# A graph network's convolution layer: W2 multiplied behind the neighbour sum, the residual product beside the last sweep

## What is computed

```python
deg = segment_sum(ones, dst); dinv = rsqrt(deg)      # with a self loop for each node
h = x @ W                                            # layer 2
agg = segment_sum(h[src] * (dinv[src] * dinv[dst])[:, None], dst) + b
x = layernorm(x + leaky(agg, 0.1) + x)
...
aggr = segment_sum(x[src] + edge_attr @ edge_w + edge_b, dst) / max(cnt, 1)     # layer 3
h = (1 + eps) * x + aggr
out = relu(h @ w1 + b1) @ w2 + b2 + (x @ res_w + res_b)
```

## Time and profile before

| | |
|---|---|
| three timed runs | 8806.70, 8809.26, 8819.43 us; median 8809.26 |
| profiled execution | 8815.13 us, span 8813.4 us |
| busy in the span | PE 2052.3 (23%), DVE 5593.5 (63%), ACT 3091.3 (35%), POOL 6086.1 (69%) |
| t2, first gather of its sums to first gather of l2s | 6208.9 to 6411.1 us |
| l2s, first to last gather | 6411.1 to 7450.2 us |
| t3, first gather to first gather of l3s | 7474.4 to 7590.0 us |
| l3s, first to last gather | 7590.0 to 8630.1 us |

### The profile page before, as it was taken

The page is one execution under the profiler, slowest core; times in us unless marked ns, Lnnn a source line. Parts: engine busy times, 40 slices in busy tenths (PEclk is TensorE's granted clock), DMA queues, the critical chain, the costliest instruction groups (busy, mean ns, idle before and its releaser), DMA issues. The chain is left out here.

```text
span 8813.4 us, 60467 instructions
## 1 busy us (share of the span) xinstructions
PE 2052.3 (23%) x16367; PEld 1898.9 (22%) x16367; DVE 5593.5 (63%) x10159; ACT 3091.3 (35%) x3341; POOL 6086.1 (69%) x6351
## 2 busy tenths in 40 slices
PE   5776634555400000810000720000500000300002
PEld 5666634555300000710000610000400000200002
DVE  7665546766599998868888468888632222432225
ACT  6333312333266665345555345555200000100002
POOL 2777777777777775667776367777267776577773
PEclk5555555555555555955555865555555555555556
DMA  4621114444366665656665556666333332233331
GB/s 131 216 60 42 37 51 134 130 133 135 115 204 219 218 216 180 206 195 216 216 216 201 170 192 216 216 216 211 93 95 105 105 105 95 78 106 105 105 105 56
DMA packets 496250, 1288.01 MB, mean 146 GB/s; under 512 B 153909, under 2 KB 262024, under 8 KB 428968
## 3 DMA queue, kind: packets, MB, share of 16 engines
q1 hardware_dynamic: 236712, 755.83, 24.3%
q0 software_dynamic: 229248, 473.78, 18.5%
q10 hardware_dynamic: 29952, 54.54, 2.4%
HBM read 731.68 MB, written 551.98 MB: 146 GB/s over the span
## 5 line engine op out<-in xcount | busy, mean ns | idle before, releaser
L1405 POOL DMA_INDIRECT l_swp_G<-table,KVI x1664 | 1576.4, 947 | 512.3 <-issue 506.7
L1661 POOL DMA_INDIRECT l2s_G<-table,OTHI x832 | 786.7, 946 | 388.1 <-issue 253.3
L1661 POOL DMA_INDIRECT l3s_G<-table,OTHI x832 | 787.7, 947 | 301.5 <-issue 253.3
L1065 POOL DMA_INDIRECT arrived<-plc_QS,plc_idx x832 | 812.3, 976 | 253.5 <-issue 244.3
L1065 POOL DMA_INDIRECT slots<-REC,plc_idx x832 | 798.5, 960 | 273.1 <-issue 251.7
L1150 POOL DMA_INDIRECT l_G<-table,OTHI x832 | 790.1, 950 | 256.1 <-issue 253.0
L904 PE MATMUL plc_pr<-plc_seen,plc_otf 128*128 128x49 f32 x3328 | 861.5, 414 | 12.4 <-DVE plc_seen L674 12.4
L904 PEld LDWEIGHTS plc_pr<-plc_seen,plc_otf 128*128 128x128 f32 x3328 | 846.6, 326 | 32.1 <-issue 31.9
L1508 DVE SCALAR_TENSOR_TENSOR l_swp_QS<-l_swp_QS,KEEP,l_swp_QX 128x128 f32<-128x128 f32 x1664 | 588.3, 354 | 45.9 <-DMA l_swp_QX<-queries 8.6
L1617 PE MATMUL l_swp_AW<-l_swp_ET,ones 128*128 128x512 f32 x4 | 4.1, 1140 | 2155.2 <-DVE l_swp_ET L1597 2155.2
L1287 DVE TENSOR_TENSOR_SCAN l_X<-l_AW,l_X 128x2244 f32<-128x2244 f32 x104 | 502.5, 4831 | 3.6
(11 more groups left out here) (491 smaller groups left out, 9633.2 us busy)
## 6 DMA issues: line engine op xcount, KB each, us to landing
sums<-l_ROW SPq DMA_DIRECT2D x104, 1088.0 KB, 4.6
l_swp_QX<-queries SPq DMA_DIRECT2D x104, 1088.0 KB, 8.3
sums<-l_swp_ROW SPq DMA_DIRECT2D x104, 1088.0 KB, 5.2
queries<-plc_zrow SPq DMA_DIRECT2D x55, 1088.0 KB
plc_QX<-queries SPq DMA_DIRECT2D x104, 544.0 KB, 4.2
l_A<-arrived SPq DMA_DIRECT2D x52, 1056.0 KB, 7.7
sums<-l3s_ROW SPq DMA_DIRECT2D x52, 1032.0 KB
plc_low<-low_rows ACTq DMA_DIRECT2D x208, 256.0 KB, 3.6
```

Of the source, the lines that this page charges most:

```text
L1065: pool.indirect_dma_start(out=slots, out_offset=bass.IndirectOffsetOnAxis(ap=idx[:, c % IB, j:j + 1], axis=0), in_=g.REC[:, c * CH + j, :] ...
L1405: pool.indirect_dma_start(out=G[:, c % GR, j, :], out_offset=None, in_=table, in_offset=bass.IndirectOffsetOnAxis(ap=index[:, c * CK + j:c ...
L1661: pool.indirect_dma_start(out=G[:, c % GR, j, :], out_offset=None, in_=table, in_offset=bass.IndirectOffsetOnAxis(ap=g.OTHI[:, c * CK + j: ...
```

## The change

Table2 now holds X * dinv rather than (X @ W2) * dinv, and the sweep sums rows without weights. In t2 the transposes, copies, products and own_rows of 49 blocks go; one pass of a group makes OWN (part 3 of norm_part), and LAG is 2. In t3 the sum, scaled and with the self loop added, is turned and multiplied by W2 with b as the bias row, and only then bent, added and normalised. The residual product moves into l3s, one block beside each chunk. To make room for its two PSUM buffers, S holds 12 slots of a chunk (SP_) instead of 16, and the sums of slots 12 to 15 are written straight to ROW. The seven passes that added b in l2s go.

```diff
+SP_ = 12
...
-        S = s.ps("S", [P, 2, CK, D])
+        S = s.ps("S", [P, 2, SP_, D])
...
+                sp.dma_start(wr[:, :], a.res_w).then_inc(loaded, 16)
+                sp.dma_start(br[:, 0, :], a.b2.rearrange("(o d) -> o d", o=1)).then_inc(loaded, 16)
+                sp.dma_start(br[:, 1, :], a.res_b.rearrange("(o d) -> o d", o=1)).then_inc(loaded, 16)
                 sp.dma_start(vec[:, :], row_of(a.edge_b)).then_inc(vec_ok, 16)
                 sp.dma_start(eps[:, :], a.eps.rearrange("(o d) -> o d", o=1).to_broadcast([P, 1])).then_inc(vec_ok, 16)
-            else:
-                sp.dma_start(vec[:, :], row_of(a.b2g)).then_inc(vec_ok, 16)
...
-                act.activation(ROW[:, c % 2, 0:CK - 1, 0:D], S[:, c % 2, 0:CK - 1, :], ACT.Copy).then_inc(rowed, 1)
+                act.activation(ROW[:, c % 2, 0:SP_, 0:D], S[:, c % 2, :, :], ACT.Copy).then_inc(rowed, 1)
+                if weight and 0 <= c - 1 < NB:
+                    n = c - 1
+                    act.wait_ge(turned, n + 1)
+                    if n >= 2:
+                        act.wait_ge(made, n - 1)
+                    act.activation(xt[:, n % 2, :], pt[:, 0:P], ACT.Copy).then_inc(copied, 1)
+                if weight and 0 <= c - 2 < NB:
+                    n = c - 2
+                    act.wait_ge(made, n + 1)
+                    act.activation(g.RES[:, n, :], pb[:, 0:D], ACT.Copy).then_inc(kept, 1)
...
             link(v.memset(ROW[:, 1, CK - 1, :], 0.0))
             if weight:
+                v.wait_ge(loaded, 48)
+                v.tensor_tensor(br[:, 0, :], br[:, 0, :], br[:, 1, :], ALU.add).then_inc(joined, 1)
                 link(v.tensor_tensor_scan(WS[:, :], g.KEEP[:, :], g.WEIGHT[:, :], 0.0, ALU.mult, ALU.add))
...
-                    line = vec[:, :].rearrange("p (o d) -> p o d", o=1).to_broadcast(wide)
                     if weight:
+                        line = vec[:, :].rearrange("p (o d) -> p o d", o=1).to_broadcast(wide)
                         link(v.tensor_tensor(g.BASE[:, cut, :], cols3(share[:, cut]).to_broadcast(wide), line, ALU.mult))
                         link(v.scalar_tensor_tensor(out=g.BASE[:, cut, :], in0=g.X[:, cut, :], scalar=eps[:, 0:1],
                                                     in1=g.BASE[:, cut, :], op0=ALU.mult, op1=ALU.add))
                     else:
                         own = g.OWN[:, cut, :]
                         link(v.tensor_tensor(own, own, cols3(g.DINV[:, cut]).to_broadcast(wide), ALU.mult))
-                        link(v.tensor_tensor(own, own, line, ALU.add))
...
-                    before = S[:, b, j - 1, :] if j else ROW[:, 1 - b, CK - 1, 0:D]
-                    after = S[:, b, j, :] if j < CK - 1 else ROW[:, b, CK - 1, 0:D]
+                    before = S[:, b, j - 1, :] if 0 < j <= SP_ else ROW[:, b if j else 1 - b, (j - 1) % CK, 0:D]
+                    after = S[:, b, j, :] if j < SP_ else ROW[:, b, j, 0:D]
...
+            def residual(n):
+                pe.wait_ge(copied, n + 1)
+                if n >= 1:
+                    pe.wait_ge(kept, n)
+                pe.matmul(pb[:, 0:D], xt[:, n % 2, :], wr[:, :], start=True, stop=False)
+                pe.matmul(pb[:, 0:D], g.ones[0:1, :], br[:, 0, :], start=False, stop=True).then_inc(made, 1)
+
+            if weight:
+                pe.wait_ge(joined, 1)
+                for n in range(NB):
+                    if n >= 1:
+                        pe.wait_ge(copied, n)
+                    pe.transpose(pt[:, 0:P], g.X[:, n, :], g.ident[:, :]).then_inc(turned, 1)
+                    if n >= 1:
+                        residual(n - 1)
+                residual(NB - 1)
             pe.wait_ge(rowed, NCK)
...
-    LAG = 11 if gcn else 3
+    LAG = 2 if gcn else 3
...
-            if gcn:
-                sp.dma_start(W2[:, :], a.W2).then_inc(rel_ok, 16)
-            else:
+            if not gcn:
...
-                n = s_ - 11
-                if gcn and 0 <= n < NB and n % GT == GT - 1:
-                    sp.wait_ge(owned, n + 1)
-                    sp.dma_start(rows(g.table2)[:, group(n // GT), :], g.OWN[:, group(n // GT), :]).then_inc(stored[0], 16)
+                G = (s_ - 8) // GT
+                if gcn and (s_ - 8) % GT == 0 and 0 <= G < NG:
+                    sp.wait_ge(owned, G + 1)
+                    sp.dma_start(rows(g.table2)[:, group(G), :], g.OWN[:, group(G), :]).then_inc(stored[0], 16)
...
-            def own_rows(n):
-                v.wait_ge(made2, n + 1)
-                v.tensor_scalar(g.OWN[:, n, :], pg[:, 0:D], g.DINV[:, n:n + 1], None, ALU.mult).then_inc(owned, 1)
+                elif j == 3:
+                    v.tensor_tensor(g.OWN[:, group(G), :], x, cols3(g.DINV[:, group(G)]).to_broadcast(wide), ALU.mult).then_inc(owned, 1)
...
-                    if 0 <= s_ - 10 < NB:
-                        own_rows(s_ - 10)
...
-            def copy_x(n):
-                act.wait_ge(turned2, n + 1)
-                if n >= 2:
-                    act.wait_ge(made2, n - 1)
-                act.activation(xt[:, n % 2, :], pf[:, 0:P], ACT.Copy).then_inc(copied2, 1)
...
-            def turn_next(n):
-                if n % GT == 0:
-                    pe.wait_ge(normed2, n // GT + 1)
-                if n >= 1:
-                    pe.wait_ge(copied2, n)
-                pe.transpose(pf[:, 0:P], g.X[:, n, :], g.ident[:, :]).then_inc(turned2, 1)
-
-            def make_own(n):
-                pe.wait_ge(copied2, n + 1)
-                if n >= 1:
-                    pe.wait_ge(owned, n)
-                pe.matmul(pg[:, 0:D], xt[:, n % 2, :], W2[:, :], start=True, stop=True).then_inc(made2, 1)
...
-                    if s_ == 8:
-                        pe.wait_ge(rel_ok, 16)
-                    if 0 <= s_ - 8 < NB:
-                        turn_next(s_ - 8)
-                    if 0 <= s_ - 9 < NB:
-                        make_own(s_ - 9)
...
-            sp.dma_start(wr[:, :], a.res_w).then_inc(loaded, 16)
-            sp.dma_start(br[:, 0, :], a.b2.rearrange("(o d) -> o d", o=1)).then_inc(loaded, 16)
-            sp.dma_start(br[:, 1, :], a.res_b.rearrange("(o d) -> o d", o=1)).then_inc(loaded, 16)
+            sp.dma_start(wr[:, :], a.W2).then_inc(loaded, 16)
+            sp.dma_start(br[:, :], a.b2g.rearrange("(o d) -> o d", o=1)).then_inc(loaded, 16)
...
             def first(G):
+                y = NV[:, group(G), :]
+                v.wait_ge(fetched[G], 16 * GT)
+                link(v.tensor_tensor(y, y, cols3(g.DINV[:, group(G)]).to_broadcast(wide), ALU.mult))
+                v.tensor_tensor(y, y, g.OWN[:, group(G), :], ALU.add).then_inc(summed, 1)
+
+            def middle(G):
                 x, y = g.X[:, group(G), :], NV[:, group(G), :]
                 m = st[:, G % 2, :, :]
-                v.wait_ge(fetched[G], 16 * GT)
-                link(v.tensor_tensor(y, y, cols3(g.DINV[:, group(G)]).to_broadcast(wide), ALU.mult))
-                link(v.tensor_tensor(y, y, g.OWN[:, group(G), :], ALU.add))
+                v.wait_ge(kept, (G + 1) * GT)
                 link(v.scalar_tensor_tensor(out=y, in0=y, scalar=0.1, in1=y, op0=ALU.mult, op1=ALU.max))
...
-            v.wait_ge(loaded, 48)
-            v.tensor_tensor(br[:, 0, :], br[:, 0, :], br[:, 1, :], ALU.add).then_inc(summed, 1)
+            first(0)
             for G in range(NG + 1):
+                if G + 1 < NG:
+                    first(G + 1)
                 if G < NG:
-                    first(G)
+                    middle(G)
                 if G >= 1:
                     second(G - 1)
...
-                act.activation(g.RES[:, n, :], pb[:, n % 2, 0:D], ACT.Copy).then_inc(kept, 1)
-
-            for G in range(NG + 1):
-                if G < NG:
-                    act.wait_ge(centered, G + 1)
-                    act.activation(SQ[:, G % 2, :, :], g.X[:, group(G), :], ACT.Square).then_inc(squared, 1)
-                if G >= 1:
-                    act.wait_ge(spread, G)
-                    act.activation(st[:, (G - 1) % 2, 2, :], st[:, (G - 1) % 2, 1, :], ACT.Sqrt).then_inc(rooted, 1)
-                if G >= 2:
-                    for n in range((G - 2) * GT, (G - 1) * GT):
-                        copy(n)
-                        if n >= 1:
-                            keep(n - 1)
-            for n in range((NG - 1) * GT, NB):
-                copy(n)
-                keep(n - 1)
-            keep(NB - 1)
+                act.activation(NV[:, n, :], pb[:, n % 2, 0:D], ACT.Copy).then_inc(kept, 1)
+
+            def close(G):
+                act.wait_ge(centered, G + 1)
+                act.activation(SQ[:, G % 2, :, :], g.X[:, group(G), :], ACT.Square).then_inc(squared, 1)
+
+            def root(G):
+                act.wait_ge(spread, G + 1)
+                act.activation(st[:, G % 2, 2, :], st[:, G % 2, 1, :], ACT.Sqrt).then_inc(rooted, 1)
+
+            for n in range(NB + 1):
+                if n < NB:
+                    copy(n)
+                if n >= 1:
```

(47 more changed lines are left out.)

## The result

| | before | changed |
|---|---|---|
| timed runs, same chip | 8808.03 us (8806.62 to 8819.43, 6 runs) | 8773.45 us (8765.52 to 8777.3, 6 runs) |
| ratio | 1 | 0.996, 95% interval 0.995 to 0.997 |
| profiled execution, span | 8813.4 us | 8771.0 us |
| t2, first gather to first gather of l2s | 202.28 us | 174.12 us |
| l2s, to the first gather of t3 | 1063.24 us | 1062.32 us |

The change is worth 34.6 us by the medians, where 34 were forecast, and 35.1 by the four stages of the two traces. The spans differ by 42.4: t2 began 7.15 us earlier in the changed kernel's execution, behind code that is the same in both. The gathers of the profiled execution of before were longer from its start (for l0, which has the same code in both, a mean of 949.6 ns against 945.1), so this belongs to the executions and to no part of the change.

A forecast was written before the change was run, and what follows sets the result against it. POOL's gathers were taken to bound the sweeps, PE's steps with waits for own_rows t2, and PE t3. The terms -30.2 (t2), -3.3 (t3), -0.6 and +0.3 (sweeps) gave -34: 8809.3 to 8775 us, range 8752 to 8792.

The forecast's parts named there:

- t2, -30.2: In t2, dropping the W2 work saves 19.0 us from keep_h(10) to keep_h(48) and 11.2 behind it.
- The clock's rival: In t2 and t3, PE is granted 0.97 for longer: -10 and -12 us, total 8753; chance 0.12.
- the ring: In t3, DVE makes the next sum only after ACT's root and scaling, and PE needs it: 12.85 us a group.
- t3, -3.3: In t3, with W2's product on every group's path, the next gather comes at 7586.7 against 7590.01: -3.3 us.
- the forecast's lower end: In t3, groups go at PE's own pace of 10.9 us, four groups 7.8 us shorter.
- The rival of a longer ring: In t3, PE stops for each square and root and groups start empty: 16 us a group, total 8791; chance 0.14.
- The sweeps, -0.3: In l2s and l3s together, ACT's shorter copy gives -0.6 us and more sums reading from SBUF +0.3.
- The gathers' rival: In both sweeps, 312 sums reading both tensors from SBUF hold gathers up 0.35 us each: +109, total 8884; chance 0.04.
- The forecast's +0.3 for the sweeps: Over both sweeps, three more sums a chunk reading from SBUF slow the gathers: +0.3 us, between 0 and +0.6.

The follow-up runs named there:

- The control kept for this on the first chip: The changed kernel itself run once more, nothing changed, on the chip where ScalarE stood still: 10228.77 us, ratio 0.9967 to the kernel before.
- the ring opened: The changed kernel with only VectorE's and ScalarE's order in t3 changed, the sum of the group after next made right behind the middle part: 8761.63 us, ratio 0.9949.
- t2 alone, again: The kernel before with W2 taken out of t2 and applied nowhere, run a second time: 8775.38 us, ratio 0.996.

## Why the prediction was right

**t2, -30.2.** Measured -28.2 in the changed kernel, and -28.5 to -34.2 in six more executions of the same t2 (173.83, 170.85, 170.59, 169.59, 168.59, 168.06 us; with the changed kernel's 174.12 the mean is 170.8, 31.5 under before). Its parts: keep_h(10) to keep_h(48) 107.56 against 108.9; a group 20.8 us against 21.1; the tail 11.1 shorter against 11.2. What was not in the sum is the stretch ahead of keep_h(10): 49.72 us before, 53.04 in the changed kernel. It is the clock. In ten executions (all but those on the first chip) the stretch took 52.65 and 53.04 us in the two that were granted 0.50 throughout, and 48.66 to 50.50 in the eight with a mean of 0.60 to 0.64, before among them. That the changed kernel's own profiled execution fell on the slower side is luck, and no part of the change. The same 20 us of t2 (20.3 us behind its first gather) in the changed kernel and in the one without the residual, whose t2 is the same code:

```profile
6222.00:6242.00 20.00, 14.59 (x58) 11.37 (x58) 12.65 (x24) 1.90 (x2) 15.77 (x14) 0.50 1.10 309
```
```profile
6225.00:6245.00 20.00, 13.20 (x72) 10.13 (x72) 15.03 (x29) 2.85 (x3) 16.04 (x14) 0.77 1.10 309
```

At a clock of 0.50 throughout (1.2 GHz) the trace has 58 matmuls in these 20 us, at 0.77, part of it at 2.4 GHz, 72, and the stretch ahead of keep_h(10) was 49.33 in place of 53.04. The control kept for this on the first chip could not decide it; the other kernels did.

**The clock's rival** (8753) did not come, and a small part of it did. In t3 the granted clock stayed at 0.50 (1.2 GHz) in every execution, with PE busy 65.87 of 82 us here and 65.48 of 72 with the ring opened. So t3 went by the row of before, as the sum had assumed. By the Trainium skill (TensorE: Matmul & The Clock Gate, Part 1) the throttled clock is the default and activity releases it; the traces of t3 do not agree. In t2 the clock moved the stage between 168.1 and 174.1 in executions of one code, and the sum's 172.1 lies between them.

**t3, -3.3.** Measured -4.0, and the layout held term by term. Seen from its first gather (7438.14) the first group is kept at 24.6 us against 24.4, the second 10.87 later against 10.9, then four groups of 12.63 against 12.85, the last 10.76 against 10.6. The tail ends at 7545.26, 10.3 us behind that, against 10.4, and the gather follows 4.5 later. Opening the ring brought the four groups to the forecast's lower end, 10.87 a group, for 7.0 us against the 7.8 of the forecast, and 1.5 more around them. The rival of a longer ring (16 us) fell because PE went on with the blocks it had while ACT made the square and the root: over those two, ACT's next product copy waits 0.17 us in place of 0.87, and its lateness is taken up.

```profile
7492.21 0.28 ACT L2422 ACTIVATE NV<-t_pb 128x128 f32<-128x128 f32 x1 [0.87 <-PE t_pb L2462]
7492.38 0.94 ACT L2426 ACTIVATE t_SQ<-X 128x896 f32<-128x896 f32 x1
7493.22 0.20 ACT L2430 ACTIVATE t_st<-t_st 128x7 f32<-128x7 f32 x1
7493.32 0.27 ACT L2418 ACTIVATE t_xt<-t_pt 128x128 f32<-128x128 f32 x1
7493.76 0.28 ACT L2422 ACTIVATE NV<-t_pb 128x128 f32<-128x128 f32 x1 [0.17 <-PE t_pb L2462]
```

**The sweeps, -0.3.** l2s 1061.71 with 15 sums in PSUM (t2 alone, again) and 1061.42 to 1062.32 in five executions with 12; l3s 1062.95 and 1062.19 to 1062.52. By the medians that is -0.2 and -0.5, the second with the residual in it. The profiled execution of before had 1063.24: its gathers were 1.6 ns longer on the mean (945.6 against 944.0), so its sweeps can't be set against those of the changed kernel to the microsecond.

**The gathers' rival** (8884) fell by its price. By the Trainium skill (SBUF — State Buffer, Who interferes with whom) a VectorE instruction with two SBUF inputs contends with a GpSimd one that reads SBUF. The runs agree, with 0.07 to 0.11 us for a whole row of 7 to 14 sums, and the change's 3 in a row cost 0.4 us in all. But the forecast's argument against this rival was wrong. It held that the attention sweep has 16 "such sums" a chunk, and those have their running sums in PSUM, so they read one large input from SBUF and bound nothing. Its median would have been no evidence either: with 14 sums from SBUF to SBUF the median did not move, and 4 to 5 us a sweep were lost. The forecast's +0.3 for the sweeps, and the 0.04 for this rival, had no row behind them; that the price is small came out of the runs, and for the prediction it was luck.

## What to carry to other kernels

When work moves from a passage to another, price the passage twice, without it and with it: here t3 was worth 30 us empty, and what moved in took 26 of them. A product put into the middle of a chain makes a ring of engines; write down who waits for whom over one group, and give each engine the work that the others wait for first, before work that only has to be done (8.6 us for an order of calls). Look for a small contention in the tail of the durations, not in their median. And before one stretch of a kernel is used as evidence for another, look up where its tiles lie: here a sum with its predecessor in PSUM was taken for one in SBUF.

## What the runs showed of the hardware

- One of the chips ran every kernel 16% slower. In t3 ACT stood there for up to 8.65 us with its product ready, and PE and VectorE waited for it, up to 37 us; the profile gives some of these waits as "issue". In l2s there VectorE's own sums stood apart too, by up to 1.5 us. The gathers of the plain sweeps took 1036 ns on the mean in place of 944. The cause isn't settled.
- VectorE's sums that read both large inputs from SBUF lengthen each gather that begins 0.10 to 0.20 us behind the start of one (301 of 301), by up to 0.13 us; sums with their predecessor in PSUM lengthen none (0 of 1068). In a row of 14 or 11 that is one gather, in a row of 7 mostly one, in a row of 3 seldom one.
- The clock granted in t2 differs between executions of the same code (20 us of it at 0.50 with PE busy 14.59 us, or at 0.77 with 13.20), and t2 with it by up to 6 us, while t3 stayed at 0.50 with PE busy 65.48 of 72 us.
- The median gather of the plain sweeps takes 944, 945 or 947 ns, by the execution and not only by the chip: on the first chip it was 944 in one trace and 947 in three, and on the last the kernel before took 8804.97 us once and 8819.95 to 8824.0 in the other eight executions.
